# Two-layer windowed-attention kernel on one Trainium2 core: the end of the tile loop and the feed-forward part written as one order

## What is computed

```python
def _layer(x, wqkv, qs, ksc, wo, lg, lb, w1, b1, w2, b2):
    h = shift_token(x)              # half of the features come from the token before
    qkv = h @ wqkv
    q, k, v = ...                   # 8 heads of 64
    q = l2norm(q) * qs
    k = l2norm(k) * ksc
    q, k = rotary_xpos(q, k)
    o = local_attention(q, k, v)    # softmax over 128 keys for each window of 64
    x = x + o @ wo
    h = shift_token(x)
    h = (h - mu) / jnp.sqrt(var + 1e-05) * lg + lb
    h = h @ w1 + b1                 # 128 -> 2 * 341
    a, g = jnp.split(h, 2, axis=-1)
    h = a * jax.nn.gelu(g, approximate=False)
    return x + h @ w2 + b2          # 341 -> 128
```

## Time and profile before

| what | us |
|---|---|
| median of 3 runs | 389.63 |
| lowest and highest | 387.52 and 389.82 |
| the profiled execution, its device time | 390.88 |
| span of the profile of that execution | 389.1 |
| mean granted PE clock | 0.98 of full speed |

### The profile page before, as it was taken

One profiled execution on the slowest core, in us unless ns is written; L12 is line 12 of the kernel. 1 busy time (PEld: TensorE's weight loads), 2 busy tenths in 40 slices (PEclk: granted clock), 3 DMA queues, 4 the chain that ended last, 5 costly groups with the idle time before them and its releaser, 6 DMA issues. The chain is left out here.

```text
span 389.1 us, 10787 instructions
## 1 busy us (share of the span) xinstructions
PE 348.4 (90%) x4007; PEld 265.4 (68%) x4007; DVE 267.7 (69%) x470; ACT 291.1 (75%) x887; POOL 257.9 (66%) x248
## 2 busy tenths in 40 slices
PE   1858779999999999988897869999999999988995
PEld 1646557888888888655454548888888888665562
DVE  4546767788878878466775676887888788365453
ACT  2556378999998999975467686899999989973620
POOL 2997479999999999720056588888998898410000
PEclk9998899999999999999999898999999999999998
DMA  6975032322322232215100122223222222200001
GB/s 192 363 153 182 3 123 56 76 56 62 72 62 49 62 77 56 49 36 182 50 0 0 28 55 47 52 63 77 55 65 62 68 58 63 60 12 7 27 27 54
DMA packets 35298, 27.63 MB, mean 71 GB/s; under 512 B 19077, under 2 KB 29231, under 8 KB 34735
## 3 DMA queue, kind: packets, MB, share of 16 engines
q1 hardware_dynamic: 34959, 26.49, 25.7%
q10 hardware_dynamic: 288, 0.46, 0.4%
HBM read 9.64 MB, written 1.05 MB: 27 GB/s over the span
## 5 line engine op out<-in xcount | busy, mean ns | idle before, releaser
L1111 ACT ACTIVATE probs<-ps,neg_max 128x128 f32<-128x128 f32 x256 | 90.0, 377 | 2.2 <-DVE neg_max L1316 1.2
L620 POOL TENSOR_TENSOR qkn<-work 128x512 f32<-128x512 f32 x64 | 80.6, 1282 | 15.4 <-DVE work L1272 5.5
L634 POOL TENSOR_TENSOR probs_n<-probs,row_inv 128x512 f32<-128x512 f32 x64 | 66.6, 1042 | 16.8 <-DVE row_inv L1321 14.6
L628 POOL TENSOR_TENSOR qkn<-qkn,rnorm 128x512 f32<-128x512 f32 x64 | 65.5, 1046 | 15.8 <-ACT rnorm L1067 15.1
L1111 ACT ACTIVATION_READ_ACCUMULATOR probs<-ps,neg_max 128x1 f32 x256 | 55.1, 215 | 0.0
L1060 ACT ACTIVATE work<-ps 128x1024 f32<-128x1024 f32 x32 | 32.8, 1026 | 22.0 <-issue 12.6
L1316 DVE TENSOR_REDUCE neg_max<-ps 128x4 f32<-128x512 f32 x64 | 41.0, 682 | 6.0 <-PE ps L834 6.0
L1262 DVE TENSOR_REDUCE ss_pair<-work 128x16 f32<-128x1024 f32 x32 | 39.0, 1220 | 8.0 <-ACT work L1060 6.1
L189 PE MATMUL ps<-wqkv_hi,h_hi 128*128 128x512 f32 x96 | 42.4, 442 | 1.6 <-ACT work L1060 1.6
L813 PE MATMUL ps<-small,qkn 128*128 128x128 f32 x256 | 37.1, 281 | 4.7 <-POOL qkn L628 4.6
L848 PE MATMUL ps<-small,probs_n 128*128 128x128 f32 x256 | 36.7, 282 | 5.1 <-POOL probs_n L634 2.8
(11 more groups left out here) (129 smaller groups left out, 758.3 us busy)
## 6 DMA issues: line engine op xcount, KB each, us to landing
v_off<-v_tok SPq DMA_DIRECT2D x64, 128.0 KB, 2.3
k_t<-k_t SPq DMA_DIRECT2D x30, 128.0 KB, 2.3
cos_w<-in_cos_t SPq DMA_DIRECT2D x2, 1024.0 KB, 8.0
sin_w<-in_sin_t SPq DMA_DIRECT2D x2, 1024.0 KB, 10.4
x_shift<-x SPq DMA_DIRECT2D x64, 32.0 KB, 1.9
x_raw<-in_x SPq DMA_DIRECT2D x4, 256.0 KB, 4.5
x<-xin SPq DMA_DIRECT2D x8, 128.0 KB, 5.5
out<-o_t SPq DMA_DIRECT2D x4, 256.0 KB, 2.3
```

What stands on the lines that cost most here:

```text
L620: pool.tensor_tensor(to, first, second[:, :, ::-1, :], ALU.add).then_inc(rot_summed, 1)
L628: pool.tensor_tensor(of, of, rnorm[:, part * HEADS:(part + 1) * HEADS].unsqueeze(2) .broadcast_to([P, HEADS, DH]), ALU.mult).then_inc(rot_ ...
L634: pool.tensor_tensor(probs_n[:, 4 * g:4 * g + 4, :], probs[:, 4 * g:4 * g + 4, :], row_inv[:, 4 * g:4 * g + 4].unsqueeze(2).broadcast_to([ ...
L1111: e = act.activation(probs[:, k, :], s_ps[g][:, cw * P:(cw + 1) * P], ACT.Exp, bias=neg_max[:, k:k + 1], accum_out=row_sum[:, k:k + 1])
```

## The change

- The loop ends with t = 14 (`over_tiles(..., TILES - 1)`). Tile 15 and the steps 15 to 17 are written out together with the feed-forward part: PE makes the first gate part of span 0 before it transposes the probabilities of tile 15, and the second and third between the last weighing and the last output projections. `centered(0)` moves to the end of step 13, `centered(1)` to the end of step 14.
- The feed-forward part runs one part ahead: PE makes the first gate part of span j+1 before it multiplies span j by w2, and both parts of a pair of PSUM banks are taken in turn (`gates`, `hidden_of`, `gelu_of`). The last normalization of a layer and its two table loads stand behind the fifth gelu.
- In layer 0 the table load, the early inverse norms and the return to the gelu table between spans 2 and 3 are gone: inverse norms of tile 16 follow the last gelu. Tile 17's squares, sum and inverse norms are now in step -1 of layer 1.
- Spans 2 and 3 of layer 1's input are rounded by ACT in four quarters of 64 x 256 each (`round_quarter`) and their rests are made by DVE (`split_quarter`): span 2's four at the end of the feed-forward part of layer 0, span 3's one at the end of each of the steps 1 to 4 of layer 1. POOL splits only spans 0 and 1.
- SP loads the cos and sin tables in step 14, behind the shift of x1 of tile 12, instead of behind the loop.
- The last span of the last layer is multiplied, added, transposed and stored in two halves of 256 tokens.

The functions that carry it, cut to their core:

```diff
-                    if layer > 0 and t == 0:
-                        pool.wait_ge(rot_scaled, 2 * n + 4)
-                        pool.wait_ge(probs_n_done, 2 * n + 2)
-                        split_input(layer, SPANS - 1)
...
-                    split_input(layer, SPANS - 2)
-                    pool.wait_ge(h_split, rounded(layer, SPANS - 2))
                 over_tiles(pool, step)
...
+                last = TILES * (layer + 1) - 1
+                scores(last, 1)
+                centered(2)
+                project_out(last - 2)
+                variance(1)
+                weigh_values(last - 1, 0)
...
+                gates(0, 0)
+                turn_probs(last, 0, True)
+                turn_probs(last, 1, True)
+                variance(2)
+                project_out(last - 1)
+                gates(0, 1)
+                weigh_values(last, 1)
+                project_out(last)
+                gates(0, 2)
+                gates(1, 0)
+                centered(3)
+                gates(1, 1)
+                variance(3)
+                feed_out(0)
+                for j in range(1, SPANS):
+                    if j > 1:
+                        gates(j, 1)
+                    gates(j, 2)
+                    if layer < LAYERS - 1 and j >= SPANS - 2:
...
+                        project_qk(layer + 1, last + 1 + j - (SPANS - 2))
+                    if j < SPANS - 1:
+                        gates(j + 1, 0)
...
+                        feed_out(j)
...
+            def round_quarter(g, q):
+                act.wait_ge(x2_done, g + 1)
+                rows, to, of = quarter(g, q)
+                act.copy(h_hi[rows, to], xin[rows, of]).then_inc(h_late_rounded, 1)
...
                     if layer > 0 and t == -1:
-                        round_input(layer, SPANS - 1)
+                        for q in range(4):
+                            round_quarter(3, q)
...
+                def split_quarter(i):
+                    dve.wait_ge(h_late_rounded, i + 1)
+                    rows, to, of = quarter(2 + i // 4, i % 4)
+                    dve.tensor_tensor(h_lo[rows, to], xin[rows, of], h_hi[rows, to],
+                                      ALU.subtract).then_inc(h_late_split, 1)
...
+                    if layer > 0 and 1 <= t <= 4:
+                        split_quarter(t + 3)
```

More of the change, by code:

```diff
@@ L38 @@
 SPANS = N // WIDE
+HALF_SPAN = WIDE // 2
 MASKED = -1e30
@@ L1147, in step @@
                         exps(n, 1)
-                    if j is not None:
-                        square(j)
                     if there(t + 1):
@@ L1204, in _ @@
-                for j in range(SPANS):
-                    span(j)
+                gelu(0, 0)
+                take_o(last)
+                gelu(0, 1)
+                gelu(0, 2)
+                gelu(1, 0)
+                square(SPANS - 1)
+                gelu(1, 1)
+                act.preload_act_table_set("natural_log_exp_and_others")
+                norm_rstd(SPANS - 1)
+                act.preload_act_table_set("gelu_and_others")
+                gelu(1, 2)
+                if layer < LAYERS - 1:
+                    round_input(layer + 1, 0)
```

436 lines of the change are left out of this document (281 added, 155 removed).

## The result

| | median, us | lowest to highest | runs |
|---|---|---|---|
| kernel before | 389.04 | 386.42 to 390.44 | 11 |
| changed kernel | 386.91 | 384.16 to 388.08 | 11 |

The ratio of the changed kernel to the one before is 0.9933 (95% interval 0.9908 to 0.9959): 2.6 us faster, between 1.6 and 3.6. The forecast was 384.7 us and a gain of 4.9. The direction and the wide range (380.4 to 387.4) hold; the forecast's own range (383.4 to 386.2) is missed, and so is the gain of over 1% to which it gave 0.70. The size is nearest to rival B. The profiled execution took 386.01 us where 386.0 was forecast, and that is luck: 3.0 us of the difference between the two profiled executions lie ahead of anything that the change touches, as the next rows show.

What follows compares the result with a forecast made beforehand. No engine full in the loop, a ring over ACT and DVE; PE's chain bounds the feed-forward part. 1.1 + 2.8 - 1.4 + 2.4 = 4.9 us gained: 386.0 profiled, 384.7 median; own range 383.4 to 386.2, wide 380.4 to 387.4.

Steps and rivals of the forecast that it cites:

- rival B: PE's waits in layer 0's feed-forward part and layer 1's first steps lower its clock: gain 3.2, 386.4 us; chance 0.17.
- Part 5: Layer 0's feed-forward part: DVE, taking turns with POOL, is the bound; ends at 213.65 against 217.7, 4.05 us won.
- Part 6: Entry of layer 1: tile 16's exponentials start 8.2 us behind PE's last product; only 1.1 of 4.05 us won are left.
- part 1: Layer 1's entry: without POOL's split of span 3, tile 17 to 18 falls from 10.23 to 7.45 us; 2.8 gained.
- Part 2: Steps 1 to 4 of layer 1: four quarters on DVE at an estimated 0.35 us each, 1.4 us lost.
- part 3: Layer 1's end of loop: overlap with the feed-forward part, product of span 0 done at 361.0 for 362.7; gain 1.65 us.
- part 4: Last span in halves: the end behind PE takes 1.3 us for 2.2, second store's issue 0.15; gain 0.75 us.
- rival A: DVE and POOL instructions do not meet in layer 0's feed-forward part and layer 1's entry: gain 9.2, 380.4 us; chance 0.18.
- C: Slower: each quarter on DVE waits for one whole POOL instruction, 1.28 us; time 392.4 us; chance 0.04.
- D: The end of the loop gives nothing, each layer loses 1.65 us: gain 1.6, time 388.0 us; chance 0.06.

Runs made afterwards that it cites:

- whole: Changed kernel with the last span of the last layer in one piece again, as before; 387.32 us, ratio 0.9966 to the kernel before.
- hold: Changed kernel with one more wait: POOL starts splitting span 0 of layer 1's input only behind the first product of span 2; 385.36 us, ratio 0.9918.
- clock run: Changed kernel with matmuls without use in PE's waits, three in layer 0's feed-forward part, two and two in layer 1's entry; 383.85 us, ratio 0.9885.
- poolq: Changed kernel with the quarters undone: POOL splits spans 2 and 3 of layer 1's input whole, ACT rounds them whole; 383.52 us, ratio 0.9873.
- spread: Changed kernel with the eight quarters on POOL instead of DVE, one in each of steps 1 to 8; 382.48 us, ratio 0.9823.
- c0: Changed kernel with the first chunk of the normalization back in step 14, centered(0) behind project_out; 385.29 us, ratio 0.9900.
- best2: best without the four matmuls without use in layer 1's entry; 378.66 us, ratio 0.9726.
- c1: c0 with the second chunk moved back too, centered(1) behind tile 15's scores; 384.77 us, ratio 0.9861.
- best: Changed kernel with eight quarters on POOL, tile 17's norms early, both chunks moved back and matmuls without use in PE's waits; 379.52 us, ratio 0.9731.

## Why the prediction was right in direction and in its wide range, and too large

The account, in us, before against "whole" up to the last sum and against after behind it:

| stretch | forecast | measured | from |
|---|---|---|---|
| to the exponentials of tile 16 (parts 5, 6) | +1.1 | +1.1 | 169.88 - 168.80 |
| from there to m17 | 0 | -1.1 | 6.75 - 7.80 |
| m17 to m22 (parts 1, 2) | +1.4 | +1.0 | 40.05 - 39.07 |
| m22 to m29 | 0 | +0.3 | 52.48 - 52.14 |
| m29 to the last sum (part 3) | +1.65 | +0.6 | 61.99 - 61.42 |
| behind it (part 4) | +0.75 | +1.2 | 4.91 - 3.74 |
| sum | 4.9 | 3.1 | |

The measured gain is 2.6 us with 1.6 to 3.6 around it. What is left may be the clock in layer 0, which fell behind PE's wait in the profile of after (0.95 us) and not in that of whole.

**Part 5 is right where its times can be read.** In before's time, `feed_out(0)`'s sum starts at 189.61 us (forecast 189.5), the third product of span 1 is done at 197.1 (196.95), PE's last product ends at 213.54 in whole (213.65). The wait was 2.67 us for 3.5, since PE got there later than I had it. "Such instructions exclude each other" held: alone 0.42 and 0.69 us, beside POOL 1.49 and 1.64. The rule of the Trainium skill, page "SBUF — State Buffer" (Terms), that on the shared port pair "the loser fully blocks", agrees with the two long ones: they ended 0.29 and 0.55 us behind the POOL instruction that each had met; rival A, which needed the meeting not to happen, falls. What the wait is worth is not settled: hold takes 2 us of it away, makes a wait of 1.46 us for POOL, and gains 0.3.

**Part 6 is right too.** Last product's end E = 210.65 + 0.8 = 211.45; the quarters end at 216.08, E+4.6 (forecast E+4.65), the exponentials start at E+8.3 (E+8.2).

**The step that failed is in part 1:** "the step falls back to 7.45 us ... nothing else in that step is late by as much". The step did fall, to 7.8 in whole. But I took it that tile 17's maxima would stand as far behind tile 16's exponentials as before, 6.75 us. They stand 7.80 behind. With the maxima of tile 16 earlier and its exponentials later, held by the quarters and by ACT's four casts, PE finds two waits of about 2 us there, and comes out of them at 1.2 GHz. That is rival B's mechanism at the second of its two places. The clock run, with 1.00 granted in both, gets 1.07 us back at this place: there the maxima stand 6.73 us behind the exponentials, as before the change. So the clock is the whole of this step's error, and the waits alone cost nothing here. The forecast had the waits ("some 2 us in the first steps of layer 1") and put them among the rivals instead of in the sum.

**Part 2:** four quarters cost 31.60 - 4 x 7.45 = 1.8 us and not 1.4. The size of the instruction was right (0.41). Two of the steps grow by 0.33, the other two by 0.57, and not for ACT: ahead of the sum of squares DVE waits 0.44 to 0.50 us for ACT's squares in all four. The short ones have the quarters of partitions 0 to 63, the long ones those of 64 to 127, where the maxima start 0.45 us behind the quarter's start instead of 0.33 and the quarter itself 0.1 later; why stays open. By poolq and spread the quarters, with those at the entry, cost 2.7 to 4.7 us up to tile 22 against the same work on POOL (spread gives 1.0 of its 4.7 back by tile 29). The removal of POOL's share, the 2.8 us of part 1, was to be had without them.

**Part 3 was mis-sized, 1.65 for 0.6.** The maxima of tile 15 come 1.7 us later instead of 1.1 (m29 to m31 17.10 for 15.44). The first gate comes 0.55 us later than forecast, 340.44 + 3.22 = 343.66 for 343.1 (3.22 is the distance of the two profiles at tile 29), in part since `hn_lo` of span 0 was held by POOL for 0.72 us (1.41 instead of 0.69) where 0.35 had been allowed. And "from there PE has no wait" is wrong by 0.65 us: the work from gates(1, 2) to the last product took 20.6 us and takes 21.3, of which 0.4 is the slower start of the matmul behind a product with w2, now counted there, and 0.3 a gap ahead of the first part of span 2. Had the first chunk stayed in step 14 (c0), part 3 would have given 1.2.

**Part 4 was mis-sized the other way,** 0.75 for 1.2. On DVE the gain is as forecast: from the last sum's start to the last output's end 1.43 us instead of 2.19. The other 0.4 us lies behind the last instruction of DVE, in the store: from issue to landing a store of 256 KB took 2.3 us before, one of 128 KB takes 1.8.

```profile
out<-o_t SPq DMA_DIRECT2D x4, 256.0 KB, 2.3
```

```profile
out<-o_t SPq DMA_DIRECT2D x2, 128.0 KB, 1.8
```

I had priced the issue, 0.15 us that no row showed, and not the transfer. The issue cost nothing: it takes 0.37 us, and the second one starts 0.6 us behind the first, when its output is ready.

**Rivals.** C (quarters held in each step) is excluded by durations of 0.41 and 0.42 in steps 1 to 4. D (the end of the loop gives nothing) came near in layer 1, 0.6 for 1.65. B was right in mechanism, and its 386.4 us is what is nearest.

What stays open: why in one execution the clock falls behind the 2.67 us in layer 0 and in another not; why it falls in spread's entry and not in best2's; and whether the 0.3 us between tiles 22 and 29 are the change. They lie in a single step of the kernel before (tile 26 to 27, 7.74 us), of which there is one profile.

## What to carry to other kernels

Ahead of pricing a removed wait, write down what the waiting engine would wait for next: hold took 2 us off one wait, made one of 1.5 us behind it and gained 0.3 us, and an early norm won 1.4 us in one step and lost 2.2 in the next. Moving work off one engine is paid where it lands; in a ring, the place in the line counts more than the amount: 0.4 us ahead of the row maxima on DVE lengthened a step, 0.7 us on POOL didn't. And waits of PE can have a second price in the clock behind them, here 1.07 us, which belongs in the sum.

## What the runs showed of the hardware

- The granted clock fell to 1.2 GHz in layer 1's entry in all five profiles with its two long waits (after, whole, hold, c0, c1; 1.87 and 2.23 us in after, with two groups of transposes of 0.63 us and a wait of 0.38 between them). It fell in the same step in spread too, where no wait was longer than 0.66 us, and not in best2, where the longest was 1.17. Behind the wait of 2.67 us in layer 0 it fell in four profiles (0.66 in after) and not in three (1.00 in whole). The length of a single wait doesn't tell it. Seven matmuls without use kept it at 2.4 GHz in the whole stretch and gained more than they cost; in best, four of them only cost.
- A DVE instruction with both inputs in SBUF, or a cast from SBUF to SBUF, that met such an instruction of POOL waited for its end. What was left behind that end was 0.13 to 0.14 us less than its own length: 0.29 us for the cast of 0.42, 0.55 for the subtraction of 0.69, 0.27 and 0.29 for the quarters of 0.41. The two engines took turns, one instruction each: four quarters and two POOL instructions took 3.70 us together. POOL's pair was held as well, 2.81 us instead of 2.50.
- Halving the last span's matmuls cost next to nothing on PE: from the first start to the last end eight pairs of 256 columns took 3.63 us, four pairs of 512 columns 3.59.
